# First attention: the row maximum of two score tiles in one instruction, its banks regrouped, and five small products moved to the other PSUM ring

## The reference

```python
qkv = x @ W_qkv                       # x: 8 x 512 x 128
q, k, v = heads of 8 features, 16 heads
scores = einsum('bhnd,bhmd->bhnm', q, k) / sqrt(128)
attn = softmax(scores, axis=-1)
out = einsum('bhnm,bhmd->bhnd', attn, v)
x = layernorm(x + out)
```

## Time and profile before

| | |
|---|---|
| median of three runs | 1043.58 us (1043.18 to 1043.74) |
| profiled execution, from its first to its last instruction | 1041.4 us |
| first attention within it, about | 13 to 403 us |
| busy over the whole span: PE, DVE, ACT, POOL | 995.5, 834.0, 729.9, 475.6 us |
| the 64 x 8 maxima of the first scores, DVE | 320.1 us busy |

### The profile page before, as it was taken

One profiled execution on the slowest core, in us unless ns is written; L12 is line 12 of the kernel. 1 busy time (PEld: TensorE's weight loads), 2 busy tenths in 40 slices (PEclk: granted clock), 3 DMA queues, 4 the chain that ended last, 5 costly groups with the idle time before them and its releaser, 6 DMA issues. The chain is left out here.

```text
span 1041.4 us, 20120 instructions
## 1 busy us (share of the span) xinstructions
PE 995.5 (96%) x5835; PEld 475.4 (46%) x5835; DVE 834.0 (80%) x1874; ACT 729.9 (70%) x939; POOL 475.6 (46%) x483
## 2 busy tenths in 40 slices
PE   8899999999999999999999999999999999999996
PEld 3222222222222235888888887873332333222485
DVE  6889999999999977787888789897666666643677
ACT  2078777787777786555555555568898888899754
POOL 0332514325053725676777677576442244220275
PEclk9999999999999999999999999999999999999998
DMA  6553222131321003344324323443512331230011
GB/s 198 153 186 119 76 76 89 44 117 46 96 78 52 3 2 101 102 128 145 101 91 156 121 90 117 137 137 102 172 65 61 121 119 63 60 122 1 1 31 52
DMA packets 73981, 97.04 MB, mean 93 GB/s; under 512 B 12669, under 2 KB 42237, under 8 KB 73533
## 3 DMA queue, kind: packets, MB, share of 16 engines
q1 hardware_dynamic: 73928, 96.40, 29.7%
HBM read 68.18 MB, written 27.79 MB: 92 GB/s over the span
## 5 line engine op out<-in xcount | busy, mean ns | idle before, releaser
L741 DVE TENSOR_REDUCE a_nmax<-a_ps_f 128x1 f32<-128x512 f32 x512 | 320.1, 683 | 20.2 <-PE a_ps_f L579 19.7
L497 ACT ACTIVATE a_prob<-a_ps_s 128x1024 f32<-128x1024 f32 x256 | 251.7, 1023 | 77.8 <-PE a_ps_s L646 76.5
L1367 ACT ACTIVATE a_prob<-a_ps_s 128x1024 f32<-128x1024 f32 x256 | 244.4, 1026 | 28.0 <-PE a_ps_s L1419 26.7
L2187 POOL TENSOR_TENSOR moe_hl<-moe_hid,moe_hh 128x512 fp32r<-128x512 f32 x134 | 173.9, 1303 | 84.3 <-ACT moe_hh L2068 84.2
L579 PE MATMUL a_ps_f<-a_ks,a_qs 48*128 48x512 bf16 x512 | 157.9, 386 | 11.8 <-DVE a_nmax L741 4.3
L2058 ACT ACTIVATE moe_ps<-moe_ps 128x512 f32<-128x512 f32 x128 | 74.5, 582 | 111.5 <-PE moe_ps L1981 110.7
L1432 PE MATMUL a_ps_o<-a_prob,a_va 128*32 128x512 f32 x1024 | 136.4, 605 | 1.4 <-DVE a_turned_o L1547 0.5
L659 PE MATMUL a_ps_o<-a_prob,a_va 128*32 128x512 f32 x1024 | 136.4, 605 | 0.5 <-ACT a_prob L497 0.4
L646 PE MATMUL a_ps_s<-a_qs,a_ks 51*128 51x512 bf16 x512 | 132.5, 381 | 1.7 <-ACT a_prob L497 1.5
L579 PEld LDWEIGHTS a_ps_f<-a_ks,a_qs 48*128 48x128 bf16 x512 | 39.7, 93 | 192.2 <-DVE a_nmax L741 162.2
L2109 DVE TENSOR_TENSOR moe_prod<-moe_cw,moe_ps 128x512 f32<-128x512 f32 x128 | 87.2, 681 | 27.4 <-PE moe_ps L1981 26.7
(11 more groups left out here) (302 smaller groups left out, 1640.1 us busy)
## 6 DMA issues: line engine op xcount, KB each, us to landing
moe_cw<-r_weights SPq DMA_DIRECT2D x256, 128.0 KB, 2.9
parts_q<-a_parts SPq DMA_DIRECT2D x48, 256.0 KB, 2.5
parts_k<-a_parts SPq DMA_DIRECT2D x48, 256.0 KB, 2.5
a_qs<-parts_q SPq DMA_DIRECT2D x126, 96.0 KB, 2.4
a_ks<-parts_k SPq DMA_DIRECT2D x126, 96.0 KB, 2.5
a_xt<-in_x_t SPq DMA_DIRECT2D x8, 256.0 KB, 2.8
out_x<-g_X SPq DMA_DIRECT2D x7, 256.0 KB, 2.3
moe_wg<-in_wg SPq DMA_DIRECT2D x1, 1088.0 KB, 6.6
```

Source lines behind the costliest of these rows:

```text
L497: nc.scalar.activation(prob[:, u % PSLOTS, :, :], ps_s[:, u % 2, :, :], ACT.Exp, scale=float(P) ** -0.5).then_inc(exp_done, 1)
L741: nc.vector.tensor_reduce(nmax[:, half_no, h % 2, col:col + 1], ps_f[:, bank, :], AX.X, ALU.max, negate=True).then_inc(max_done, 1)
L1367: nc.scalar.activation(prob[:, u % PSLOTS, :, :], ps_s[:, u % 2, :, :], ACT.Sigmoid, scale=float(HD) ** -0.5).then_inc(exp_done, 1)
L2187: nc.gpsimd.tensor_tensor(hl[:, part_at(j), :], hid[:, hid_at(j), :], hh[:, part_at(j), :], ALU.subtract).then_inc(hl_done, 1)
```

## The change

First, `ps_f` is used in two ways in turn: groups of two first scores in banks 0 and 1, and groups of one in bank 2. There are 44 groups a batch (`first_groups`): 22 pairs, 20 singles, and the two halves of the turned output at the places of singles 5 and 31. DVE takes the maxima of a pair with one instruction over 128 x 2 x 512. PE waits with a group until the group two places earlier has been read, that is, a pair waits for the pair ahead of it.

Second, v, q, k and both turned maxima leave the `ps_f` ring. They take slots of the `ps_s` ring, behind the last work of a unit: v and the second turned maxima together behind unit 6, q behind 13, k behind 17, the first turned maxima behind 23 (`take_guests`). A unit that follows a guest then has the slot of the unit just ahead of it.

The scores are spread over the 64 half units as groups (`groups_of`); the maxima lie in `nmax` in their order, and POOL's `split_max` reads them with a stride of two. `stats` moves from the first score 16 to unit 8, which is the same place.

```diff
-V_AT, Q_AT, K_AT = 16, 25, 33
-MT_AT = (47, 11)
-OT_AT = (46, 9)
-STATS_AT = 16
+HALF_N = S1_N // 2
+N_GROUPS = 44
+O1_GROUP, O0_GROUP = 5, 31
+STATS_U = 8
+V_AT, Q_AT, K_AT, MAX0_AT = 6, 13, 17, 23
...
+def first_groups():
+    groups, n = [], 0
+    for k in range(N_GROUPS):
+        if k == O1_GROUP:
+            groups.append("o1")
+        elif k == O0_GROUP:
+            groups.append("o0")
+        else:
+            size = 2 - k % 2
+            groups.append(tuple(range(n, n + size)))
+            n += size
+    return groups
+def bank_of(k):
+    return 2 * (k % 2)
+def groups_of(u, second):
+    at = lambda h: -(-N_GROUPS * h // (2 * NU))
+    return range(at(2 * u + second), at(2 * u + second + 1))
+SLOTS = [x for u in range(NU) for x in [u] + [t for t, at in (("v", V_AT), ("q", Q_AT), ("k", K_AT), ("max0", MAX0_AT))
+                                              if at == u]]
+def slot_of(turn):
+    return SLOTS.index(turn) % 2
...
-                nc.tensor.matmul(ps_f[:, BANK["qk"[n]], :], w[:, n, :], xt[p][:, :], start=True,
+                nc.tensor.matmul(ps_s[:, slot_of("qk"[n]), 0, :], w[:, n, :], xt[p][:, :], start=True,
...
+                elif back if turn[0] < LATE else fore:
+                    free_bank(b, k)
+                    for i, t in enumerate(turn):
                         score_b, n = score_of(t, b - 1)
+                        s1(score_b, 1 - p if t < LATE else p, n, bank_of(k) + i)
...
+                if u == V_AT and (fore or back):
+                    free_slot(b, "v")
+                    if back:
+                        turn_max(b - 1, 1)
                     if fore:
+                        v_product(b, p)
+                if u == Q_AT and qk_on:
+                    free_slot(b, "q")
+                    qk_product(b + 1, 1 - p, 0)
+                if u == K_AT and qk_on:
+                    free_slot(b, "k")
+                    qk_product(b + 1, 1 - p, 1)
+                if u == MAX0_AT and fore:
+                    free_slot(b, "max0")
+                    turn_max(b, 0)
...
-                pe.wait_ge(exp_done, NU * b + u - 1 + EXP_C)
+                free_slot(b + 1, u)
...
-                        for t in turns_of(u, second):
-                            take_turn(b + 1, 1 - p, t, qk_on, fore, back, tail)
+                        for k in groups_of(u, second):
+                            take_group(b + 1, 1 - p, k, fore, back, tail)
+                    take_guests(b + 1, 1 - p, u, qk_on, fore, back)
...
-                dve.wait_ge(s1_done, S1_N * b + n + 1)
-                nc.vector.tensor_reduce(nmax[:, half_no, h % 2, col:col + 1], ps_f[:, bank, :], AX.X, ALU.max,
-                                        negate=True).then_inc(max_done, 1)
+                dve.wait_ge(s1_done, S1_N * b + n + count)
+                nc.vector.tensor_reduce(nmax[:, half_no, at:at + count], ps_f[:, bank:bank + count, :], AX.X, ALU.max,
+                                        negate=True).then_inc(max_done, count)
```

More of the change, by code:

```diff
@@ L76, with group_exists, group_before, score_of @@
                "sin": [P, T]}
[L78 to L85, removed]
+def first_groups():
[10 more added lines that the diff above has]
+    return groups
+GROUPS = first_groups()
+def bank_of(k):
+    return 2 * (k % 2)
+def group_exists(k, b):
+    if not isinstance(b, int):
+        return True
+    turn = GROUPS[k]
+    if turn == "o1":
+        first, last = 2, NB
+    elif turn == "o0":
+        first, last = 1, NB
+    elif turn[0] < LATE:
+        first, last = 1, NB
+    else:
+        first, last = 0, NB - 1
+    return first <= b <= last
+def group_before(k, b):
+    for back in range(2):
+        for q in range(k - 1 if back == 0 else N_GROUPS - 1, -1, -1):
+            if bank_of(q) == bank_of(k) and group_exists(q, b - back):
+                return q, back
+    return None
+def groups_of(u, second):
+    at = lambda h: -(-N_GROUPS * h // (2 * NU))
+    return range(at(2 * u + second), at(2 * u + second + 1))
+def score_of(n, b):
+    return (b, n + S1_N - LATE) if n < LATE else (b + 1, n - LATE)
+SLOTS = [x for u in range(NU) for x in [u] + [t for t, at in (("v", V_AT), ("q", Q_AT), ("k", K_AT), ("max0", MAX0_AT))
+                                              if at == u]]
+def slot_of(turn):
+    return SLOTS.index(turn) % 2
+def slot_exists(turn, b):
     if not isinstance(b, int):
@@ L89, in exists, with slot_before @@
     if isinstance(turn, int):
-        first, last = (1, NB) if turn < LATE else (0, NB - 1)
+        first, last = 1, NB
     else:
-        first, last = {"q": (0, NB - 2), "k": (0, NB - 2), "v": (0, NB - 1), "max0": (0, NB - 1),
-                       "o1": (2, NB)}.get(turn, (1, NB))
+        first, last = {"q": (0, NB - 2), "k": (0, NB - 2), "v": (0, NB), "max0": (0, NB - 1)}[turn]
     return first <= b <= last
[L97 to L104, removed]
+def slot_before(turn, b):
+    at = SLOTS.index(turn)
     for back in range(2):
[L106 to L109, removed]
-    return None
[L113 to L121, removed]
+        for q in range(at - 2 if back == 0 else len(SLOTS) - 2 + at % 2, -1, -2):
+            if slot_exists(SLOTS[q], b - back):
+                return SLOTS[q], back
+    return None
 def is_first(b):
@@ L364, in out_bank @@
         def out_bank(b, n):
-            return 0 if is_last(b) else BANK[f"o{n}"]
+            return 0 if is_last(b) else bank_of((O0_GROUP, O1_GROUP)[n])
         front = Front(nc, g, m, ps_f[:, 1, :], ps_f[:, 2, :], xt)
@@ L599, in take_turn @@
[L599 to L604, removed]
-                        score_b, n = score_of(t, b - 1)
-                        s1(score_b, 1 - p if t < LATE else p, n, BANK[t])
-                elif t == "v":
+                    pe.wait_ge(exp_done, NU * (b - 1) + t + 1 + EXP_C)
+                elif t == "v":
+                    if not (isinstance(b, int) and b == NB):
+                        pe.wait_ge(v_taken, b + 1)
+                    if not (isinstance(b, int) and b == 0):
+                        pe.wait_ge(mt_copied, 2 * b)
+                elif t == "max0":
+                    pe.wait_ge(mt_copied, 2 * b + 1)
+                else:
+                    pe.wait_ge(q_taken if t == "q" else k_taken, b + 2)
```

135 lines of the change are left out of this document (64 added, 71 removed).

## The result

The changed kernel takes 1059.65 us (median of four runs, 1058.74 to 1062.14), the kernel before 1043.41 in the same comparison. The ratio is 1.0158, with a 95% interval of 1.0143 to 1.0172: slower by 16 us. The profiled execution took 1062.14 us, the slowest of the four, with a span of 1060.5.

The account below looks back on a forecast made before the run. DVE was taken as the bound. A batch of 39.9 work, 3.5 at V's and 2.7 for guests makes 46.1 us against 44.16; seven batches add 13.3, the lead-in 1.0, giving 1058 us, likeliest 1050 to 1067, range 1040 to 1067.

Parts of the forecast that it names:

- Fewer maxima: DVE's first-score maxima: a pair's step is 1.14 us, its end 1.22; DVE's work falls 1.3 us a batch.
- Banks that come free later: DVE's stock across each V: idle of 3.5 us a batch in place of 1.3, so 2.2 more.
- its maximum can start 0.42 later: First scores: DVE can start a maximum 0.42 us after PE starts its score, used for pairs too.
- Guests: Products for q, k, v and turned maxima and outputs: 2.7 us a batch in place of 1.7, so 1.0 more.
- these and for what q leaves late: v's product, the turned maxima and outputs, and q's late remainder: 0.6 us a batch, between 0 and 1.1.
- At no cost: Exponentials on ACT, POOL's strided reads, earlier turning and SP's loads are hidden and add nothing.
- a guest without cover: Score ring: were the exponential's wait not hidden by a product on PE, each of four guests would cost up to 1 us.
- Ahead of batch 0, and at the ends: Lead-in before batch 0, where PE runs fillers: 1.0 us more in all, from 0 to 2.4.
- Rival 1 (guests hidden): q, k and v run while PE would wait for a maximum anyway: batch 43.4 us, time 1038; chance 0.10.
- Rival 2 (refill in time): DVE's stalls stay at 1.3 and 1.7 us: batch 42.9, time 1035, or 1023 with stalls gone; chance 0.08.

Follow-up runs that it names:

- run 6: The changed kernel with DVE taking the maxima of a pair by two instructions of 512 elements in place of one: 1057.98 us, ratio 1.014.
- run 7: The changed kernel with a pair's maximum raising its counter by one in place of two, PE and POOL waiting for the number of maxima: 1054.12 us, ratio 1.0104.
- run 1: The changed kernel's guests (v, q, k, turned maxima) in the score ring, but single maxima over three banks as before: 1055.82 us, ratio 1.0116.
- run 3: Single maxima over three banks, guests in the score ring, with q and k behind units 12 and 16 in place of 13 and 17: 1055.5 us, ratio 1.01.
- run 4: Single maxima, guests in the score ring, v, q and k between the two first scores of units 6, 12 and 16: 1052.01 us, ratio 1.0075.
- run 8: The changed kernel with the first half's group issued ahead of the second scores in even units: 1054.52 us, ratio 1.0096.
- run 2: The changed kernel with the product for k issued twice in the same place, the second overwriting the first with the same numbers: 1064.98 us in one run.
- run 9: The changed kernel with q and k behind units 12 and 16, counter updates by one, and first scores ahead of second scores in even units: 1044.9 us, ratio 1.0025.

## Why the prediction was right, and which terms were off

The time was predicted at 1058.0 (1040 to 1067) and measured at 1059.65. The mechanism held: DVE leads, its work fell, and its waits for PE grew by more, with the longest at the product for k and the next at that for q. A batch was put at 46.1 and took 46.95. In its own terms:

| term, us a batch | predicted | measured |
|---|---|---|
| DVE's work: 22 pairs, 20 singles, divisions, statistics | 39.9 | 39.85 |
| idle behind the V's, the one at k left out | 3.16 | 3.7 |
| guests, with the V at k | 3.06 | 3.0 |
| division behind the turned output | 0 | 0.4 |
| sum | 46.1 | 46.95 |

The measured column is read from the steps of DVE in batch 3 (194.83 to 241.74): what a step takes beyond 1.142 us for a pair and 0.598 for a single is lost, that is an idle time and some 0.07 to 0.09 of overlap with it. A V near a guest is counted with what a V of its kind loses elsewhere, and the guest with the rest.

*Fewer maxima.* A pair's step of 1.14 us and its end at 1.22 were hit. The work saved is 22 x (2 x 0.598 - 1.142) = 1.2 us, and 0.054 us for each merge. The Trainium skill (Perfetto Trace Analysis, section Optimizing Scalar/DVE Operations) gives 125 ns of overhead for a DVE access to PSUM, which by estimate was 2.75 us a batch; the trace doesn't agree, with 0.054 us in the step from one start to the next. Of the 1.2 us, run 6 against run 7 showed 0.36 to arrive.

*Banks that come free later.* Right in mechanism, and the term that was mis-sized: 3.16 predicted, 3.7 measured. The step that failed is "its maximum can start 0.42 later", which was read from singles. A pair starts 0.52 behind its scores (216.48 to 217.00). So a V with a pair behind its second scores cost 0.47 in place of 0.36 (the wait of 0.39 at 210.47, and 0.08 of overlap), and one with a pair right behind it 0.25 in place of 0.14 (the 0.17 at 203.25). Against that, the V ahead of the statistics cost nothing, since DVE has these to do. Run 7 shows 0.06 of the 0.10 to be the update by two, which the prediction had nowhere. Three runs that differ in one thing each take this part of the change apart: from single banks (run 1, 46.21) to banks in pairs, read one by one (run 6, 46.74) 0.53 is lost; the merged read (run 7, 46.38) gains 0.36; the update by two (46.95) loses 0.57.

*Guests.* 3.06 predicted, 3.0 measured. The product for q lost 1.10 (1.0 predicted; 1.01 idle and 0.09 of overlap), the one for k with its V 1.35 (1.42). For "these and for what q leaves late" 0.6 was taken; v lost 0.37, and what q and k leave late at the next V is 0.08 and 0.09. That the sum agrees is in part luck: the same moves without merged maxima (run 1) lose 2.05, 0.4 of it by the division, where the prediction had 1.0. The difference lies mostly at the V behind v, which waits 0.62 there; in the changed kernel the statistics fall at that V. So the losses of the two parts don't simply add. A product that empties DVE's stock can be paid a second time at the next V, and runs 3 and 4 showed that this depends on how many first scores stand between the two.

*At no cost.* In batches 1 to 5 of the changed kernel no matmul waits for an exponential, and no trace shows a cost of POOL or SP; theory B of run 4, which would have made the score ring the cause, fell. Not at no cost was the turned output, which the prediction had left at its place: it now stands right behind a V, and the division waits for it. DVE, then PE:

```profile
200.47 0.36 DVE L812 RECIPROCAL a_rec<-a_ps_f 128x32 f32<-128x32 f32 x1 [0.34 <-PE a_ps_f L728]
...
198.69 1.07 PE L720 MATMUL a_ps_o<-a_prob,a_va 128*32 128x512 f32 x8
199.69 0.66 PE L728 MATMUL a_ps_f<-g_ident,moe_dsb 128*128 128x128 f32 x4
```

Nor were the exponentials free in batch 7, where no product covers them. PE waits for one ahead of the second turned maximum (L602) in its slot of the score ring, and for another behind it:

```profile
388.05 0.26 PE L602 MATMUL a_ps_s<-a_identb,a_msplit 128*96 128x128 bf16 x1 [0.50 <-ACT a_prob L544]
388.96 0.39 PE L707 MATMUL a_ps_s<-a_qs,a_ks 51*128 51x512 bf16 x2 [0.66 <-ACT a_prob L544]
```

From unit 6 to unit 8 the exponentials of batch 7 fall back by 1.3 of its 1.5 us, and by as much in runs 1, 6, 7 and 8, which have the same slot. It is the cost that the prediction named for a guest without cover; it had counted on cover everywhere.

*Ahead of batch 0, and at the ends.* Predicted +1.0, measured -1.3, below the range of 0 to 2.4. The clock is part of it. The windows of before, then of the changed kernel (columns as in the earlier trace rows, with the granted clock behind the five engines):

```profile
42.00:46.00 4.00, 4.00 (x12) 0.84 (x12) 2.08 (x4) 0.27 (x1) 0.00 (x0) 0.57 0.56 181
```

```profile
38.00:42.00 4.00, 3.02 (x15) 1.02 (x15) 2.99 (x4) 0.27 (x1) 2.70 (x6) 1.00 0.44 149
42.00:46.00 4.00, 4.00 (x17) 1.07 (x16) 3.69 (x5) 0.00 (x0) 0.00 (x0) 1.00 0.40 130
52.83:55.80 2.97, 1.59 (x10) 0.30 (x6) 2.65 (x3) 2.66 (x3) 0.00 (x0) 1.00 1.00 396
55.80:62.60 6.80, 6.36 (x27) 0.96 (x27) 4.02 (x5) 3.27 (x4) 4.01 (x5) 0.50 0.86 342
```

Before, PE was busy 1.37 of 4.00 us, and then its granted clock fell (0.57 over the next 4 us). In the changed kernel the turned maxima come earlier, PE is busy 3.02 of those 4 us, and the clock stays. It fell instead at 55.8, to 0.50 (1.2 GHz), behind 52.83 to 55.80 with PE busy 1.59 of 2.97, and lay in batch 0, which took 48.08. Run 2, without such a stretch, had batch 0 at 46.25, of which 0.86 is its second product: some 2.7 us of the 48.08 are the clock. The prediction has these nowhere, nor the 1.5 in batch 7. It has 7 x 1.9 + 1.0 = 14.3 for the span, against 19.1 in the profiled execution, which took 2.5 us more than the median. That the total came within 2 us of 1058 is partly luck: batches 1 to 5 were taken too cheap by 0.85 each, batch 6 and the stretch ahead of batch 0 too dear by 1.4 and 2.3. It also added 2.2 us for what lies around the span, where the profiled execution has 1.6 (1062.14 - 1060.5). What moves the clock's fall from one stretch to the other was not tried; that PE idled ahead of each is all that the rows show.

*The rivals.* Rival 1 (guests hidden) is wrong by run 2: 0.86 us more of PE are 0.86 more of waiting. Rival 2 (refill in time) is wrong by the waits, 25.4 us in five batches where it kept 7.1. With q and k at other places and the small losses gone (run 9) the change only ties. Two kernels were not tried: pairs with the guests left in the ring of the first scores, and run 9 with single maxima; so it stays open whether the pairs could win with all else at its best.

## What to carry to other kernels

An instruction that reads two buffers of a ring gives them both back late: weigh the work it saves against the stock that its reader loses, and count that stock in the reader's time, not in buffers. Long work on the engine that fills the ring belongs where most items stand ahead of it, and far from the next long work; moved by one unit, two products of 1.06 us were worth 2 us of 47 here. Before merging anything, try the moves that the merge needs by themselves, and see whether the merged instruction has taken on something else, here an update by two that cost more than the merge gained.

## What the runs showed of the hardware

A maximum over 1024 elements of PSUM takes one step of 1.14 us, two over 512 take 1.20: back to back, an instruction costs DVE only 0.054 us.

An update by two delays its own instruction: pairs started 0.52 us behind their scores, 0.46 with an update by one, in the same order of work (run 7); a single starts 0.42 behind its score (223.17 to 223.59). With the update by two the wait stands as an EVENT_SEMAPHORE of its own in DVE's queue, 22 in a batch, and a batch is 0.57 us longer. The Trainium skill (Trainium Kernel Development and Optimization, section Key Constraints) says that the semaphores of compute engines rise by 1. In this kernel a rise by two worked, at that cost.
